# A 16-batch graph-attention kernel: the loop over batch pairs on every engine replaced by straight code with constant waits

## What is computed

```
h = maximum(layernorm(x), 0)
q, k, v = h @ Wq + bq, h @ Wk + bk, h @ Wv + bv        # per head: 64 columns
scores = q @ k.T / sqrt(64) + where(adj == 0, -1e9, 0)
out = x + softmax(scores) @ v
```

## Time and profile before

| | us |
|---|---|
| median of 3 runs | 4096.61 |
| the profiled execution | 4094.8 |
| its span | 4093.0 |
| TensorE (PE) busy | 4027.1 (98%) |
| VectorE busy | 3100.4 (76%) |
| ScalarE busy | 3075.5 (75%) |
| GpSimd busy | 1394.2 (34%) |
| idle of PE put down to "issue" before L571 | 14.6, in 6 pieces |
| granted TensorE clock, mean | 0.996 |

### The profile page before, as it was taken

The page is one execution under the profiler, slowest core; times in us unless marked ns, Lnnn a source line. Parts: engine busy times, 40 slices in busy tenths (PEclk is TensorE's granted clock), DMA queues, the critical chain, the costliest instruction groups (busy, mean ns, idle before and its releaser), DMA issues.

```text
span 4093.0 us, 77408 instructions
## 1 busy us (share of the span) xinstructions
PE 4027.1 (98%) x22016; PEld 3279.4 (80%) x22016; DVE 3100.4 (76%) x5128; ACT 3075.5 (75%) x5514; POOL 1394.2 (34%) x1409
## 2 busy tenths in 40 slices
PE   7999999999999999999999999999999999999998
PEld 6888888878887888878888788887888878888886
DVE  6877878777777777768777687776877868778686
ACT  5877868778686786867868688686886868868687
POOL 4333333333333333323333333332333333333322
PEclk9999999999999999999999999999999999999999
DMA  5232322322222222223222232222322323223121
GB/s 181 69 92 63 85 65 77 86 66 83 80 64 84 72 82 81 62 80 84 70 81 70 73 91 62 81 80 63 92 65 77 84 57 92 77 65 92 44 73 47
DMA packets 240106, 316.30 MB, mean 77 GB/s; under 512 B 16400, under 2 KB 147472, under 8 KB 231056
## 3 DMA queue, kind: packets, MB, share of 16 engines
q1 hardware_dynamic: 239632, 310.71, 26.6%
HBM read 172.23 MB, written 37.75 MB: 51 GB/s over the span
## 4 chain that ended last, share of the span: by engine, by line
PE 81%; issue 9%; POOL 5%; DMA 2%; ACT 2%; SPq 1%; DVE 0%; POOLq 0%; ACTq 0%; DVEq 0%
PE T L559 18%; PE misc L517 14%; PE S L547 10%; PE S L548 10%; PE O L571 10%; PE O L578 10%; PE misc L530 8%; DMA xln<-in_x 1%; POOL kB L400 1%; POOL kA L400 1%; PE misc L587 1%; PE misc L496 1%; POOL xln L381 1%; ACT y L670 1%; POOL outs L420 1%
## 5 line engine op out<-in xcount | busy, mean ns | idle before, releaser
L847 DVE TENSOR_TENSOR pT<-T,pT 128x512 fp32r<-128x512 f32 x2048 | 1390.7, 688 | 712.5 <-ACT pT L679 699.7
L679 ACT CAST pT<-T 128x512 fp32r<-128x512 f32 x2048 | 1185.5, 590 | 671.1 <-PE T L559 573.6
L841 DVE CUSTOM_DVE_ANT_0 S<-S,mask 128x1024 f32<-128x1024 f32 x1024 | 1257.2, 1228 | 9.0 <-PE S L548 8.1
L559 PE MATMUL T<-ident,probs 128*128 128x128 f32 x8192 | 1233.9, 273 | 0.6 <-DVE pT L847 0.2
L559 PEld LDWEIGHTS T<-ident,probs 128*128 128x128 f32 x8192 | 1005.1, 140 | 279.7 <-DVE pT L847 36.4
L687 ACT ACTIVATE probs<-S,negmax 128x1024 f32<-128x1024 f32 x1024 | 1151.6, 1125 | 8.3 <-DVE negmax L841 5.1
L578 PE MATMUL O<-pT,vs 128*64 128x512 f32 x2048 | 965.6, 471 | 0.2 <-DVE pT L847 0.2
L571 PE MATMUL O<-pT,vs 128*128 128x512 f32 x2048 | 816.9, 399 | 14.7 <-issue 14.6
L517 PE MATMUL misc<-hT,wqk 128*128 128x512 f32 x3036 | 789.7, 395 | 4.3 <-ACT y L670 0.8
L517 PEld LDWEIGHTS misc<-hT,wqk 128*128 128x128 f32 x3036 | 557.0, 188 | 156.5 <-ACT y L670 18.4
L420 POOL TENSOR_TENSOR outs<-outs,oT 64x512 f32<-64x512 f32 x256 | 331.7, 1296 | 560.8 <-DMA outs<-oT 539.7
(11 more groups left out here) (70 smaller groups left out, 3590.3 us busy)
## 6 DMA issues: line engine op xcount, KB each, us to landing
wqk<-wqk_split SPq DMA_DIRECT2D x63, 1024.0 KB, 6.5
xln<-in_x SPq DMA_DIRECT2D x240, 256.0 KB, 2.6
outs<-in_x SPq DMA_DIRECT2D x66, 512.0 KB, 4.5
kA<-kA SPq DMA_DIRECT2D x128, 256.0 KB, 3.2
kB<-kB SPq DMA_DIRECT2D x128, 256.0 KB, 3.9
outs<-oT SPq DMA_DIRECT2D x256, 128.0 KB, 3.4
out<-outs SPq DMA_DIRECT2D x64, 512.0 KB, 4.0
probs<-in_adj SPq DMA_DIRECT2D x4, 1024.0 KB, 5.0
```

The costliest lines, as they stand in the source:

```text
L559: mm = pe.transpose(T[:, u % 2, i * P:(i + 1) * P], probs[:, (GB * g + i) % RING, j * P:(j + 1) * P], ident[:])
L679: act.copy(pT[:, u % PT, 0, :], T[:, u % 2, :]).then_inc(p_hi, 1)
L841: dve.tensor_tensor_reduce(S[:, s % 2, :], S[:, s % 2, :], mask[:, s % NB, :], 1.0, 3.0e38, ALU.add, ALU.min, negmax[:, s % RING:s % RING ...
L847: dve.tensor_tensor(pT[:, u % PT, 1, :], T[:, u % 2, :], pT[:, u % PT, 0, :].bitcast(F32), ALU.subtract).then_inc(p_lo, 1)
```

## The change

The loop on each of the five engines becomes `for b in range(1, B - 1): body(b)`, executed when the program is built. The bodies are the same functions, now called with a number, so each batch has its own instructions with constants in its waits and addresses. The three `..._passed` semaphores and their increments go. No compute instruction and no DMA is added, removed or moved.

```diff
-        dve_passed, gp_passed, sp_passed = sem("dve_passed"), sem("gp_passed"), sem("sp_passed")
...
             def load_xln(b, t):
 
-                sp.sem_inc(sp_passed)
                 sp.dma_start(xln[:, t % XLN, :], x[b, t * P:(t + 1) * P, :]).then_inc(xln_in[t % XLN], 16)
...
             def move_o(b, g):
...
                 sp.wait_ge(o_copied, n + 1)
-                sp.sem_inc(sp_passed)
                 used = 2 * (PAIRS * b + g // 4) + half - 1
                 if some(used):
                     sp.wait_ge(o_turned, used)
-                    sp.sem_inc(sp_passed)
...
             body(0, first=True)
-            with sp.Fori(0, B // 2 - 1) as two:
-                body(2 * two + 1)
-                body(2 * two + 2)
+            for b in range(1, B - 1):
+                body(b)
             body(B - 1, last=True)
...
                 gp.wait_ge(ln_part, 3 * (NB * b + (t + 1 if some(b) else t // 2 * 2 + 2)))
-                gp.sem_inc(gp_passed)
                 tile = x_tile(b, t)
                 gp.tensor_scalar(tile, tile, negmean[:, t:t + 1], rstd[:, t:t + 1],
...
             body(0, first=True)
-            with pe.Fori(0, B // 2 - 1) as two:
-                body(2 * two + 1)
-                body(2 * two + 2)
+            for b in range(1, B - 1):
+                body(b)
             body(B - 1, last=True)
...
                 dve.wait_ge(scored, n + 1)
-                dve.sem_inc(dve_passed)
                 dve.tensor_tensor_reduce(S[:, s % 2, :], S[:, s % 2, :], mask[:, s % NB, :], 1.0,
```

More of the change, by code:

```diff
@@ L478, in _ @@
             body(0, first=True)
-            with gp.Fori(0, B // 2 - 1) as two:
-                body(2 * two + 1)
-                body(2 * two + 2)
+            for b in range(1, B - 1):
+                body(b)
             body(B - 1, last=True)
@@ L787, in _ @@
             body(0, first=True)
-            with act.Fori(0, B // 2 - 1) as two:
-                body(2 * two + 1)
-                body(2 * two + 2)
+            for b in range(1, B - 1):
+                body(b)
             body(B - 1, last=True)
@@ L921, in _ @@
             body(0, first=True)
-            with dve.Fori(0, B // 2 - 1) as two:
-                body(2 * two + 1)
-                body(2 * two + 2)
+            for b in range(1, B - 1):
+                body(b)
             body(B - 1, last=True)
```

## The result

The changed kernel takes 4067.13 us (median of 4 runs, 4064.13 to 4069.8) beside 4096.68 for the kernel before (4 runs, 4095.68 to 4097.57). The ratio is 0.9929, with a 95% interval of 0.9915 to 0.9943: some 30 us less, 0.7%. The profiled execution took 4066.34, its span is 4064.5 (before: 4093.0).

A forecast was written before the change was run, and what follows sets the result against it. TensorE, busy 98% of the span, was taken to bound the kernel. 4094.8 - 24.5 - 6.6 + 5.9 - 0.3 = 4069.3, with 1.8 for the runs' median 4071 us; range 4061 to 4082.

The forecast's parts named there:

- The jumps: TensorE's six loop back edges, at the L571 matmul, cost 4.1 us each in idle and low clock; gain 24.5 us.
- (B): Straight stream pauses at many points of TensorE's stream, or half the back edges' time returns elsewhere; 4083 us, 7%.
- (C): At the back edges clock and refill are lost anyway, only the visible holes go; 4079.5 us, 7%.
- (E): The jump itself costs next to nothing, the holes are periodic and stay; 4095.6 us, no change, 2%.
- The x tiles: Stall of the L496 transposes at slot 85, behind SyncE's load, falls from 10.1 to 3.5 us; gain 6.6.
- Rival (D): The x-tile chain gets worse, its phase against kB's landings being new; 4083 us, 6%.
- Constants on TensorE: Waits on constants in TensorE's formerly looped batches cost a net 0.42 us a batch, +5.9 us over 14.
- Rival (A): Constant form costs at every TensorE place with several waits; 4150 us, a loss from 2.2 us a batch; 3%.
- Late landings of kB: Late kB in some looped batches, four counted, 1.9 us, left as they are; could move the time -2 to +4.
- Prologue and tail: The parts outside the 14 looped batches lose the increments too; gain 0.3 us.

The follow-up runs named there:

- e3: Kernel before with seven batches per loop turn, so one jump back in place of six; 4075.9 us, ratio 0.9957.
- e4: Kernel before with only TensorE still looping, the four other engines written out, increments kept; 4090.3 us, ratio 0.9981.
- e6: Changed kernel with a five-turn loop of one semaphore increment added on TensorE ahead of batches 3, 5, ... 13; 4068.3 us, ratio 0.994.
- e2: Kernel before with one batch per loop turn, so 13 jumps back in place of six; 4094.1 us, ratio 1.0001.
- e10 to e12: Kernel before with 64, 128 and 192 useless instructions at the start of TensorE's program; 4078.6, 4085.4 and 4090.0 us beside 4096.15.
- e7: Changed kernel with the late wait, for the misc bank, named first in the q, k and v projections; 4055.5 us, ratio 0.9895.
- e1: Kernel before with only the loops written out on all five engines, semaphore increments kept; 4070.9 us, ratio 0.9946.
- e9: Changed kernel with the late wait first in the projections and x tile 3's load ahead of the copies of k; 4049.3 us, ratio 0.9885.
- e5: Kernel before with only TensorE written out, the four other engines still looping, increments kept; 4081.7 us, ratio 0.996.

## Why the prediction was right

The forecast of 4071 us was 4 us from the measured 4067.1. The mechanism was right, and the number is closer than its terms: some were too large and some too small. Step by step, for the 14 batches (27.05 us in the profiles):

- **The jumps, 24.5 predicted.** Right: every boundary runs like the one of batches 0 and 1. Slots 112 to 127 before the jumps and 0 to 15 after them had taken 24.8 us more than where no jump stands, and now take nothing more. e3, e4 and e6 show that it is TensorE's far jump. What the prediction left open, why a jump costs 4.1 us, turned out to be in good part an accident of placement (e2, e10 to e12). Rivals (B), (C) and (E) are out: no holes inside the batches, and the clock came back with the holes.
- **The x tiles, 6.6 predicted.** 5.1 measured: the idle at slot 85 of batches 1 to 14 fell from 10.1 to 4.9, not 3.5. Twelve batches have 0.02 to 0.44, but batch 1 has 1.04, with a load whose issue took SyncE 2.01 us in place of 0.67, and batch 4 has 1.68, where the data landed 5.5 us after the issue in place of 4. Rival (D) happened in two batches of fourteen. The trace offers a cause: in both, an instruction packet of TensorE's queue was in flight with the load. Of the 180 such loads in the twelve kernels that issue them behind the copies of k, 28 had company of that kind. TensorE waited 1.2 us on average after those and 0.5 after the others, and all 14 waits over 1.15 us are among the 28. No run tested it by itself.
- **Constants on TensorE, +5.9 predicted.** +4.7 measured, the 47 waits being 3.8 of it: a batch without the slot-85 idle is 251.0 us in place of 250.7. Slots 16 to 127 are 0.5 us longer, as batch 0 had shown, and slots 0 to 15 0.1 to 0.2 shorter. e7 confirmed the reason. Rival (A) asked for 2.2 us a batch.
- **Late landings of kB, 0 predicted.** 1.9 gained: none of the 14 batches had one. The seven kernels with TensorE written out have none, and four of the seven with TensorE in a loop have two to five. Why was not tried.
- **Prologue and tail, 0.3 predicted.** 1.4 measured. The miss is in batch 0's first slots: they took 39.66 us in the kernel before and 38.54 after, and the granted clock over the stretch 58 to 68 us goes with it, in the kernel before, then after:

```profile
58.00:68.00 10.00, 8.26 (x25) 5.90 (x26) 5.61 (x10) 6.38 (x12) 0.00 (x0) 0.66 0.65 227
```

```profile
58.00:68.00 10.00, 7.68 (x29) 5.40 (x30) 6.42 (x11) 6.50 (x12) 0.30 (x1) 0.83 0.65 230
```

This 1.1 us is not the change's: e1, with the increments, has 38.52, e2 and e4, with TensorE in a loop, 38.55 and 38.53, and e9, which is straight and has no increments, 39.62 and the low clock for as long as the kernel before. It came into the result by chance.

Sum: -24.8 - 5.1 + 4.7 - 1.9 = -27.1, against 27.05 measured. Against the prediction's terms, 1.5 us less came from the x tiles, and 1.2, 1.9 and 1.1 us more from the constants, kB and the prologue.

The Trainium skill's figure of about 108 ns for a compare-and-branch (Advanced Engine Details and Errata, Control Flow Timing) is near the branch that falls through, 76 to 83 ns, and half of the short jumps' 213; it is no price for a far jump, which took 3.4 to 5.2 us. The Trainium skill (Runtime: NRT & Kernel Launch, Instruction fetch mechanics) states that a taken jump out of the fetched window has to wait until its target's page is fetched. The trace agrees: every far branch, 4.8 us in the kernel before, ended after an instruction packet that had started during it, and of e6's 24 short jumps none took over 0.4 us.

## What to carry to other kernels

Compare the same slots of peeled and looped batches in one profile before writing anything: it priced the jumps, the constants and the stall to within 2 us each. A back edge over long code cost TensorE 1.3 to 4.7 us here, depending on where the jump stood in the stream, and the dear ones often cost the clock as well, so look for matmuls that start at twice their distance behind it, and count the instruction packets. Before you credit a change with a wait that appears in the list, remember that the list has a lower limit. In hand-written waits, name first the one that lands last, so that the instruction carries it, and let no load that is ready stand in a queue behind a copy that is not.

## What the runs showed of the hardware

- The price of a jump back depends on its place in the instruction stream: 64 instructions more at the start of the program took the branch from 4.8 to 3.5 us, TensorE's hole from 2.4 to 1.0, and with the shorter hole the clock did not fall, so that a jump cost 1.3 us in place of 4.1. In e2 the target stands where it does in the kernel before and the jump does not (the distance differs too), and the first hole is 1.1 against 2.4. In all 13 far jumps with a branch of 4.7 us or more (the kernel before, e3, e4) two instruction packets start during the branch, and in all 31 with 3.4 to 4.2 us (e2, e10 to e12) one.
- The second hole, before L528 or L530, is the next packet. It comes at each of e2's 13 jumps (0.47 to 1.01 us), at two of six in the kernel before (0.56) and at two in e4 (0.83 and 1.11), 3.0 to 3.6 us after the branch, and ends 1.2 to 1.5 us after that packet has landed, as the branch does after its own. It occurs in none of the 18 jumps with a shifted target, and in none where the clock fell, where the matmuls took longer.
- The clock: of 13 holes of 2.2 to 2.8 us (the kernel before, e3, e4) nine were followed by the 1.2 GHz level; the other four are those with a second hole. The 31 holes of 0.8 to 1.6 us (13 in e2, 18 in e10 to e12) were followed by it at none. Six stalls of 2.0 to 2.3 us at slot 85 were followed by it at three (e3 twice, e6 once) and not at three (e5 twice, e6 once), so between 2.0 and 2.8 us the length of the hole alone does not decide.
- SyncE's pause of 0.35 us between the copies of k, in the even batches of the kernel before and e5, has an instruction packet of q14 beside it each time, 0.8 us after the load that follows; the odd batches have neither.
